# Edge sum of a graph layer: three fields a list in place of four, and VectorE's dependent operations spaced out

## The chip, the cores and the metric
One core of one Trainium2 chip runs the whole kernel. The metric is the device time of one execution in microseconds, the median over runs. The engines are TensorE (PE; PEld is its weight load), VectorE (DVE), ScalarE (ACT), GpSimd (POOL) and the sync engine (SP), which only issues transfers.

## The reference, cut to what matters
```python
# x: (6250, 256) f32; src, dst: (200000,) sorted by dst; edge_weight: (200000,) f32
xn = layernorm(x)
row, col = src, dst                       # edge_index = stack([src, dst])
gnn = segment_sum(edge_weight[:, None] * xn[col], row, num_segments=6250) + node_vec1
x = x + gnn + linear_attention(xn)        # four heads of 64, no softmax
x = x + mixture_of_experts(layernorm(x))  # 8 experts, the best 2 of each row
```
The edge sum is the part at issue: every edge adds its weight times the normalized row of `dst` to the row of `src`. Its weights are 32-bit floats and are kept in full in the sum.

## The kernel before, in words
The nodes are 49 tiles of 128 rows. `front` normalizes the rows, computes what the attention needs and prepares the edges; `edge_sum` adds up the edges and the attention; `stragglers`, `route` and `experts` follow. The change touches `front` and `edge_sum`.

**Edges as lists.** Since the edges are sorted by `dst`, those of one tile of `dst` lie together. Tile s of `dst` takes a window of 34 x 128 edges (CH = 34 per partition). Sorting one such window, called sort s, puts its edges into a table of 128 slots by NB = 49 tiles of `src`: one *list* per tile of dst, with one edge per slot and tile of src. It is done by one-hot products. `hot_t` (L1121) marks each edge's src tile, `base` (L845, 34 matmuls of 49 columns) counts the edges ahead, `rank_ahead` and `rank` (L1134 to L1145) give each edge its slot, `slots` (L1153) marks it. `values` (L1164) multiplies `hot_t` by each *field* of the edge, spread by ACT's `repeat_fields` (L981) over 1666 elements. `make_table` (L854) multiplies slots by values, 34 matmuls of FIELDS x 49 columns into one PSUM bank. ACT's `unpack` or `unpack_list` copies it out, and DVE's `part` (L1172, L1173) or `make_list` (L1180 to L1186) takes the fields apart.

**Fields.** There are four bf16 fields: END packs the two row numbers, and three hold the weight as a sum of bf16 parts, each the rest after the one before. In `front`, `weight_part` (POOL, five steps a chunk of seven tiles, one per node tile from APART on) makes the three parts with copies and subtractions, and `apart` (DVE, L547 to L559) the END field.

**Use of the lists.** The 49 tiles of dst make seven groups of seven. In a group four lists are *dense* (DENSE; src side is a one-hot block matrix times a resident window of xn rows) and three are *pick* lists (PICK; for them POOL gathers one row of xn per slot from DRAM, L817). For each group, all 49 tiles of src are computed, seven to a *unit*. So there are 7 x 49 node-tile steps in 49 units. In a step PE makes `blocks` of the next tile (L903, 12 bf16 matmuls of 128 columns) from DVE's `hots` (L1284) and `hot_w` (L1288, three weight parts), and `rows` (L911 and L915, seven f32 products of 256 columns); ACT copies the blocks out (`evacuate`, L1027) and spreads the next unit's entries (`take`, L1015 to L1021); DVE makes `pick_w` (`picks`, L1295) and adds the sum to the result (`add`, L1316).

**What sets the order.** Each engine runs one queue written out by hand: `schedule` runs eight sorts first (with the attention's `mix` between), then 42 units that each carry one more sort spread over their steps i = 0 to 6, then seven units without. In a unit's step i DVE does `picks` of tile i+1, `hots` with `hot_w` of tile i+2, `add` of tile i-1, then a piece of the sort: two `values` at 0, `part`, `in_row`, `rank_ahead` at 1, `rank` at 2, `make_list` and one `values` at 3, one at 4, `slots` at 5, `hot_tiles` at 6. PE does `base` at 0 and `make_table` at 6. Waits between engines are on counting semaphores; DVE also waits on its own semaphore where an operation reads what the one before wrote:
```python
dve.tensor_tensor(to ..., ALU.is_equal).then_inc(hot_done, 1)      # hots, L1284
dve.wait_ge(hot_done, t + 1)
dve.tensor_tensor(hot_w[i % SETS] ..., ALU.mult).then_inc(w_done, 1)  # L1288
```

Of the kernel before, what the change touches and what calls it, by code (L numbers as in the profile page):

```python
# [22 lines left out]
P = 128  # L23
# [20 lines left out]
FIELDS = 4  # L44
END, W = 0, 1
# [132 lines left out]
def front(nc, shared, edges, mixing, x, node_vec1, wq, wk, wv, wo, bo, kg, kb, vg, vb, xn_dram, xT_dram, src, dst, edge_weight,  # L178
# [25 lines left out]
    with ExitStack() as ctx:  # L204
# [7 lines left out]
        dst_t, src_t, dst_r, src_r = (sb(name, [P, UN, CH], I32) for name in ("dst_t", "src_t", "dst_r", "src_r"))  # L212
# [86 lines left out]
        def _(pool):  # L299
# [16 lines left out]
            def weight_part(c, n):  # L316

                at, part = slice(c * UN, (c + 1) * UN), n // 2
                if n == 0:
                    pool.wait_ge(e_in[c], 16 * 3 * UN)  # L320
                else:
                    pool.wait_ge(parts, 5 * c + n)
                if n % 2 == 0:
                    pool.tensor_copy(fields[:, W + part, at, :], weight[:, at, :]).then_inc(parts, 1)
                else:
                    pool.tensor_tensor(weight[:, at, :], weight[:, at, :], fields[:, W + part, at, :], ALU.subtract).then_inc(parts, 1)

            chunk_root(0)
            for t in range(NT):
                c, i = divmod(t, UN)  # L330
                root(t)
                if i == 2 and c + 1 < NC:
                    chunk_root(c + 1)
                for k in range(NC):
                    if 1 <= t - APART[k] <= 5:
                        weight_part(k, t - APART[k] - 1)
# [115 lines left out]
        def _(dve):  # L452
# [81 lines left out]
            def apart(c, m):  # L534

                at = slice(c * UN, (c + 1) * UN)
                if m == 0:
                    dve.wait_ge(e_in[c], 16 * 3 * UN)
                    if c > 0:
                        dve.wait_ge(kept, 2 * c)  # L540
                if m < 4:
# [8 lines left out]
                elif m == 4:  # L550
                    dve.wait_ge(cut, 4 * c + 3)
# [64 lines left out]
def edge_sum(nc, shared, edges, mixing, hot_w, xn_dram, xT_dram, base_dram, sum_dram, z_dram, Wg, bg, bias, wg, gb_row, G, NG, NT, N, D, HD):  # L616
# [16 lines left out]
    PARTS = FIELDS - W  # L633
# [5 lines left out]
    with ExitStack() as ctx:  # L639
# [23 lines left out]
        pair = sb("pair", [P, NB])  # L663
# [59 lines left out]
        listed = sem("listed"); pick_done = sem("pick_done"); rows_in = [sem(f"rows_in{i}") for i in range(SETS)]  # L723
# [82 lines left out]
        def _(pool):  # L806
            pool.wait_ge(mix_added, (GRP - 1) * BU)
            for t in range(NG * NT):
                g, b = divmod(t, NT)
                i = t % BU  # L810
                if b == 0:
                    pool.wait_ge(listed, 3 * PICK * (g + 1))
# [141 lines left out]
        def _(act):  # L954
# [22 lines left out]
            def repeat_fields(s, a, b):  # L977

                if later(s):
                    act.wait_ge(vals_done, 3 * s - (2 if b <= 2 else 1 if b <= 3 else 0))  # L980
# [17 lines left out]
            def unpack(s, j, par):  # L998
# [3 lines left out]
                act.copy(at[:, :, :, bass.ds(j, 1)].rearrange("p b f a -> p (f a) b"), table_ps).then_inc(unpacked, 1)  # L1002

            def unpack_list(s, n, q, par):
# [3 lines left out]
                if later(n):  # L1008
                    act.wait_ge(listed, 3 * n)
# [19 lines left out]
            def sort(s):  # L1029
                take_base(s)  # L1030
                repeat_fields(s, 2, 3)
                repeat_fields(s, 3, FIELDS)
# [6 lines left out]
                repeat_fields(s + 1, 0, 2)  # L1039

            def begin():
                act.wait_ge(unpacked, GRP)
                act.wait_ge(parted, DENSE)
                act.wait_ge(listed, 3 * PICK)
# [4 lines left out]
            def unit(g, k, odd, par, turn, more, after, q):  # L1049
# [4 lines left out]
                for i in range(BU):  # L1054
# [9 lines left out]
                    if more and i == 0:  # L1064
# [4 lines left out]
                        take_base(s)  # L1069
                        repeat_fields(s, 2, 3)  # L1070
                    if more and i == 1:
                        repeat_fields(s, 3, FIELDS)
                    if after and i in (2, 4):
                        if turned:
                            act.wait_ge(unpacked, (g + 2) * GRP)
                            act.wait_ge(parted, (g + 2) * DENSE)
                            act.wait_ge(listed, (g + 2) * 3 * PICK)
# [9 lines left out]
                    if more and i == 6:  # L1087
                        repeat_fields(s + 1, 1, 2)
# [8 lines left out]
            repeat_fields(0, 0, 2)  # L1097
# [3 lines left out]
        def _(dve):  # L1101
# [34 lines left out]
            def rank(s):  # L1136

                dve.wait_ge(ahead_done, 3 * s + 1)
                dve.wait_ge(same_done, s + 1)
                dve.tensor_tensor(ahead[:, :, 0:CH], ahead[:, :, 0:CH], same[:, :, :], ALU.add).then_inc(ahead_done, 1)  # L1140
                dve.wait_ge(ahead_done, 3 * s + 2)
                dve.tensor_tensor(ahead[:, :, 0:HALF], ahead[:, :, 0:HALF], ahead[:, :, NB + 1 - HALF:NB + 1], ALU.add).then_inc(ahead_done, 1)
                dve.wait_ge(ahead_done, 3 * s + 3)
# [23 lines left out]
            def part(s, j, par):  # L1167
# [5 lines left out]
                dve.tensor_scalar(both, both, P - 1, 0x3F80, ALU.bitwise_and, ALU.bitwise_or).then_inc(parted, 1)  # L1173

            def make_list(s, n, q, par):
# [5 lines left out]
                dve.tensor_scalar(row[:, :], raw[:, END, :].bitcast(I32), 23, None, ALU.logical_shift_right).then_inc(listed, 1)  # L1181
                dve.tensor_tensor(pair[:, :], raw[:, W, :], raw[:, W + 1, :], ALU.add).then_inc(listed, 1)
                dve.wait_ge(listed, 3 * n + 2)
                dve.tensor_tensor(place[par][:, bass.ds(q, 1), :].rearrange("p a b -> p (a b)"), row[:, :],
                                  first_row[:, bass.ds(s, 1)].broadcast_to([P, NB]), ALU.add)
                dve.tensor_tensor(weight[par][:, :, bass.ds(q, 1)].rearrange("p b a -> p (a b)"), pair[:, :], raw[:, W + 2, :], ALU.add).then_inc(listed, 1)  # L1186
# [56 lines left out]
            def sort(s):  # L1243
# [16 lines left out]
                values(s, 0, 2)  # L1260
# [4 lines left out]
                values(s, 2, 3)  # L1265
                if later(s):
                    add_mix(t + 1)
                values(s, 3, FIELDS)
                hot_tiles(s + 1)
                if later(s):  # L1270
                    add_mix(t + 2)
                slots(s)
                if s % 2 == 1:
                    part(s - 1, (s - 1) // 2, 0)
                elif s > 0:
                    make_list(s - 1, s // 2 - 1, s // 2 - 1, 0)

            def hots(t, i, odd, free):

                if free is not None:  # L1280
# [5 lines left out]
                                  of[:, i, 0:HOTS, :].unsqueeze(2).broadcast_to([P, HOTS, RUNS, REP]), ALU.is_equal).then_inc(hot_done, 1)  # L1286
                dve.wait_ge(hot_done, t + 1)
# [11 lines left out]
            def begin():  # L1299
# [3 lines left out]
                hots(0, 0, 0, None)  # L1303
                picks(0, 0, 0)
                hots(1, 1, 0, None)
                dve.wait_ge(saved, 16 * GRP)

            def unit(g, k, odd, par, turn, more, after, q):
# [13 lines left out]
                for i in range(BU):  # L1322
                    if i + 1 < BU:
# [792 lines left out]
```

## Time and profile before
| | us |
|---|---|
| median of 3 runs | 2283.73 (2283.42 to 2287.97) |
| profiled execution, its span from the first to the last instruction | 2536.7 |
| busy in it: PE, DVE, POOL, ACT | 2230.1, 1963.9, 1551.1, 1174.3 |
| mean granted TensorE clock | 0.929 |

The profiled execution has no time of its own beside its span. What lies around the span is not shown, and the span is 253 us longer than the median, so durations are read from single instructions and the span is not compared with the median directly. By time, the front runs to about 180 us, the eight sorts to 300, the 42 units with a sort to 1815, the seven without to 2060, routing and experts behind.

### The profile page before, as it was taken

How to read it: one execution, taken by the hardware profiler on the slowest of the kernel's cores; microseconds unless marked ns; L12 is line 12 of the kernel's file. 1: busy time of each engine (PE TensorE's matmuls, PEld its weight loads, DVE VectorE, ACT ScalarE, POOL GpSimd, SP SyncE). 2: the span in 40 equal slices, each digit the busy share in tenths (PEclk: the TensorE clock that was granted, in tenths of full speed). 3: DMA queues.
4: the chain of work that ended last, by engine and by line, in shares of the span. 5: the costliest groups of instructions: out<-in, count | busy, mean ns of one | idle time of the engine just before them, and what ended most of it. 6: DMA issues, size and time to landing. Idle time of an engine off the chain costs nothing. (4 is left out here: it accounts for less than half of the span.)

```text
span 2536.7 us, 45539 instructions
## 1 busy us (share of the span) xinstructions
PE 2230.1 (88%) x16549; PEld 1930.5 (76%) x16550; DVE 1963.9 (77%) x3350; ACT 1174.3 (46%) x1696; POOL 1551.1 (61%) x1356
## 2 busy tenths in 40 slices
PE   7987799999999899989988998999989944999993
PEld 4656687777887788778877787778877844999993
DVE  7989888788898788878877897879877757555552
ACT  2236544443444344434443454444322235888772
POOL 4750266666676566666665666666766612778883
PEclk9989999999999899989988999999999977999997
DMA  5532422222223222222222222222244453455555
GB/s 151 150 113 87 123 82 75 76 90 78 74 83 90 73 82 76 88 76 80 76 82 73 83 79 84 78 79 77 82 123 139 136 180 61 79 81 83 82 81 133
DMA packets 160931, 235.90 MB, mean 93 GB/s; under 512 B 54834, under 2 KB 121805, under 8 KB 160490
## 3 DMA queue, kind: packets, MB, share of 16 engines
q0 software_dynamic: 70896, 164.43, 25.4%
q1 hardware_dynamic: 75536, 55.29, 7.9%
q10 hardware_dynamic: 14314, 13.68, 1.6%
q8 instruction: 120, 1.97, 0.3%
q14 instruction: 65, 0.53, 0.1%
HBM read 186.46 MB, written 53.24 MB: 94 GB/s over the span
## 5 line engine op out<-in xcount | busy, mean ns | idle before, releaser
L817 POOL DMA_INDIRECT picked<-xn_dram,place x1029 | 1143.9, 1112 | 721.7 <-PE bank L915 289.8
L1027 ACT COPY stage<-bank 128x512 f32<-128x512 f32 x343 | 201.0, 586 | 796.9 <-remote 477.6
L915 PE MATMUL bank<-picked,pick_w 128*128 128x256 f32 x2058 | 518.4, 389 | 3.3 <-issue 3.3
L915 PEld LDWEIGHTS bank<-picked,pick_w 128*128 128x128 f32 x2058 | 405.7, 197 | 65.8 <-issue 5.2
L911 PE MATMUL bank<-window,stage 128*128 128x256 f32 x1568 | 416.9, 409 | 17.8 <-issue 12.8
L903 PE MATMUL bank<-hot_w,hots 128*128 128x128 bf16 x4116 | 312.0, 225 | 49.1 <-issue 44.8
L911 PEld LDWEIGHTS bank<-window,stage 128*128 128x128 f32 x1568 | 300.4, 202 | 65.1 <-issue 25.6
L1164 DVE TENSOR_TENSOR vals<-hot_t,field_rep 128x1666 bf16<-128x1666 bf16 x200 | 203.7, 1041 | 187.8 <-remote 180.2
L1288 DVE TENSOR_TENSOR hot_w<-hots,cur 128x1536 bf16<-128x1536 bf16 x343 | 328.6, 958 | 11.9
L903 PEld LDWEIGHTS bank<-hot_w,hots 128*128 128x128 bf16 x4116 | 267.1, 101 | 92.5 <-issue 54.5
L911 PE MATMUL bank<-stage 128*128 128x256 f32 x1176 | 315.5, 410 | 11.6 <-issue 10.4
L981 ACT COPY field_rep<-fields 128x1666 bf16<-128x1666 bf16 (+1 forms) x193 | 322.8, 1677 | 1.2 <-DVE vals L1164 1.2
L1284 DVE TENSOR_TENSOR hots<-ends,cur 128x1408 bf16<-128x1408 bf16 x343 | 303.1, 884 | 1.7 <-ACT cur L1021 1.7
L911 PEld LDWEIGHTS bank<-stage 128*128 128x128 f32 x1176 | 225.9, 203 | 49.0 <-issue 23.2
L1908 POOL DMA_INDIRECT sum_dram<-y,target x112 | 179.1, 1599 | 64.0 <-issue 31.1
L1316 DVE TENSOR_TENSOR acc<-acc,bank 128x256 f32<-128x256 f32 x343 | 142.3, 415 | 85.2 <-PE bank L915 44.7
L1295 DVE TENSOR_TENSOR pick_w<-hots,cur_w 128x384 f32<-128x384 bf16 x343 | 190.6, 556 | 0.2
L1899 POOL DMA_INDIRECT zin<-z_dram,token x112 | 115.5, 1031 | 83.4 <-POOLq L1600 49.6
L2002 PE MATMUL bank<-w,hh 128*128 x896 | 163.6, 282 | 1.1 <-DVE hl L2050 1.1
L854 PE MATMUL bank<-vals,slot 128*128 128x196 bf16 x1700 | 155.8, 249 | 4.9 <-issue 4.0
L854 PEld LDWEIGHTS bank<-vals,slot 128*128 128x128 bf16 x1700 | 147.9, 98 | 12.3 <-issue 5.8
L2002 PEld LDWEIGHTS bank<-w,hh 128*128 128x128 f32 x896 | 138.2, 189 | 1.4 <-issue 1.4
(253 smaller groups left out, 3414.6 us busy)
## 6 DMA issues: line engine op xcount, KB each, us to landing
picked<-xn_dram,place POOLq DMA_INDIRECT x1029
w<-in_L_ffn_W_dram SPq DMA_DIRECT2D x16, 512.0 KB, 8.9
xn_dram<-xn ACTq DMA_DIRECT2D x49, 128.0 KB, 1.9
xT_dram<-xT ACTq DMA_DIRECT2D x49, 128.0 KB, 2.1
base_dram<-acc SPq DMA_DIRECT2D x7, 896.0 KB
sum_dram<-acc SPq DMA_DIRECT2D x7, 896.0 KB
z_dram<-vals SPq DMA_DIRECT2D x7, 896.0 KB
out_dram<-sum_dram SPq DMA_DIRECT2D x1, 6250.0 KB, 21.8
```

Source lines behind the costliest of these rows:

```text
L817: pool.indirect_dma_start(out=picked[:, i % SETS * PICK + q, :], out_offset=None, in_=xn_dram, in_offset=bass.IndirectOffsetOnAxis(ap=plac ...
L854: mm = pe.matmul(table_ps, slot[:, c, :], vals[:, c, :, :], start=(c == 0), stop=(c == CH - 1))
L903: mm = pe.matmul(block_ps(pp, j), hot[buf][:, PICK + j, :], hot_w[buf][:, part, j, :], start=(part == 0), stop=(part == 2))
L911: pe.matmul(sum_ps[pp], block_sb[pp][:, j, :], window[par][:, j, :], start=(j == 0), stop=False)
L915: mm = pe.matmul(sum_ps[pp], pick_w[i % SETS][:, q, :], picked[:, i % SETS * PICK + q, :], start=False, stop=(q == PICK - 1))
L981: act.copy(field_rep[:, :, a:b, :], fields[:, a:b, bass.ds(s, 1), :].rearrange("p f a c -> p (a c) f").unsqueeze(3).broadcast_to([P, CH, b ...
L1027: act.copy(block_sb[pp].rearrange("p j c -> p (j c)"), banks[pp][:, :]).then_inc(a_copied, 1)
L1164: ins = dve.tensor_tensor(vals[:, :, f, :], hot_t[:, :, :], field_rep[:, :, f, :], ALU.mult)
L1284: dve.tensor_tensor(to[:, :, :].rearrange("p f (b r) -> p f b r", r=REP), ends[:, :, :].rearrange("p f (b r) -> p f b r", r=REP), of[:, i, ...
L1288: dve.tensor_tensor(hot_w[i % SETS][:, :, :, :].rearrange("p f g (b r) -> p f g b r", r=REP), to[:, AT_SRC:HOTS, :].rearrange("p g (b r) - ...
L1295: dve.tensor_tensor(pick_w[i % SETS][:, :, :].rearrange("p q (b r) -> p q b r", r=REP), hot[i % SETS][:, 0:PICK, :].rearrange("p q (b r) - ...
L2002: mm = pe.matmul(y_ps[i][:, n * D:(n + 1) * D], parts[a][:, c, n * P:(n + 1) * P], w, start=(m == 0), stop=(m == 3 * FC - 1))
```

## The change
A list has three fields: END, W and LOW. W is now the upper 16 bits of the weight, taken as they are. LOW holds the lower 16 bits with bit 14 taken out and a constant added (so that the pattern is an ordinary bf16 number); the bit taken out goes to the END field's free upper bit. After the table, DVE puts the bits together again (`halve`, `join`). For a dense list it then cuts the joined weight into the three bf16 parts that `hot_w` reads (`part_cut`, `part_weights`); for a pick list the joined word is the weight. The table's matmuls have 147 columns, and `hot_w` keeps its three parts.

In `front`:
```diff
-FIELDS = 4
+FIELDS = 3
 # weight_part (POOL): three steps in place of five
+high = weight[:, at, :]....bitcast(U16)[:, 1:2 * UN * CH:2]
+pool.tensor_copy(fields[:, W, at, :].bitcast(U16)..., high).then_inc(parts, 1)
+pool.wait_ge(cut, 6 * c + 2)
+pool.tensor_scalar(fields[:, LOW, at, :].bitcast(U16), low_k[:, :, :], float(LOWEST * P), None, ALU.add).then_inc(parts, 1)
+pool.wait_ge(cut, 6 * c + 6)
+pool.tensor_tensor(src_r[:, :, :], src_r[:, :, :], bit_e[:, :, :], ALU.add).then_inc(parts, 1)
 # apart (DVE), m == 0
+dve.tensor_scalar(low_k[:, :, :], bits, 0xBFFF, None, ALU.bitwise_and).then_inc(cut, 1)
+dve.tensor_scalar(bit_e[:, :, :], bits, 0x4000, 1, ALU.bitwise_and, ALU.logical_shift_left).then_inc(cut, 1)
 # m == 5
-dve.wait_ge(cut, 4 * c + 4)
+dve.wait_ge(parts, 3 * c + 3)
```
In `edge_sum`, ACT:
```diff
 def unpack(s, j, par):
-    act.copy(at[:, :, :, bass.ds(j, 1)]..., table_ps).then_inc(unpacked, 1)
+    act.copy(at[:, :, 0:2, bass.ds(j, 1)]..., table_ps[:, END:W + 1, :])
+    raw_free(s)
+    act.copy(raw[:, :, :], table_ps).then_inc(unpacked, 1)
 def unpack_list(s, n, q, par):
+    act.copy(weight[par][:, :, bass.ds(q, 1)]..., table_ps[:, W, :])
+    raw_free(s)
     act.copy(raw[:, :, :], table_ps).then_inc(unpacked, 1)
 # unit: repeat_fields(s, 1, 2) at i == 0, (s, 2, 3) at 1, (s + 1, 0, 1) at 3, none at 6
```
DVE:
```diff
+def halve(s):
+    dve.tensor_scalar(halves[:, 0, :], raw[:, LOW, :].bitcast(I32), 16, None, ALU.logical_shift_right)
+    dve.tensor_scalar(halves[:, 1, :], raw[:, END, :].bitcast(I32), 17, 0x4000, ALU.logical_shift_right, ALU.bitwise_and).then_inc(split, 1)
+def join(s, low_bits):
+    dve.wait_ge(split, splits_of(s) + 1)
+    return dve.scalar_tensor_tensor(out=low_bits, in0=halves[:, 0, :], scalar=float(-LOWEST * P), in1=halves[:, 1, :], op0=ALU.add, op1=ALU.add)
+def part_cut(s):
+    dve.wait_ge(split, splits_of(s) + 2)
+    dve.tensor_scalar(upper[:, :], raw[:, W, :].bitcast(I32), 8, 8, ALU.logical_shift_right, ALU.logical_shift_left).then_inc(split, 1)
+def part_weights(s, j, par):
+    dve.wait_ge(split, splits_of(s) + 3)
+    dve.tensor_tensor(second, upper[:, :].bitcast(F32), first, ALU.subtract)
+    dve.tensor_tensor(third, raw[:, W, :], upper[:, :].bitcast(F32), ALU.subtract).then_inc(parted, 1)
 # make_list: row and halve; place_list: join and place; pair and the sum into weight are gone
 # unit, step i
-picks(t + i + 1, ...)
-hots(t + i + 2, ...)        # with hot_w behind its own wait
-add(i - 1)
+hots(t + i + 2, ...)
+picks(t + i + 1, ...)
+rank_add(s), part_cut(s - 1)      # at i == 2
+weigh(t + i + 2, ...)             # hot_w
+rank_fold(s)                      # at i == 2
+add(i - 1)
+rank_sum(s)                       # at i == 2
```
The sort's other pieces in a unit's step, each behind `add`: one `values` at 0; at 1 `part` with `halve`, `in_row`, `part_join`, `rank_ahead`; at 3 `part_weights` or `make_list`, one `values`, `place_list`; one `values` at 4; `slots` and `hot_tiles` as before. In the eight sorts ahead of the units, `part` or `make_list` stands behind the last `values`, and `join`, `cut` and `part_weights` are spread between `hot_tiles`, `add_mix` and `slots`. The semaphore `listed` counts one per pick list in place of three, `parted` is counted by `part_weights`.

## Rows read from the trace of the kernel before
**Rows 1.** The page: its span, and part 1, busy time by engine.
```profile
span 2536.7 us, 45539 instructions
...
PE 2230.1 (88%) x16549; PEld 1930.5 (76%) x16550; DVE 1963.9 (77%) x3350; ACT 1174.3 (46%) x1696; POOL 1551.1 (61%) x1356
```

**Rows 2.** Stretches: length, busy PE, PEld, DVE, ACT, POOL, granted clock, DMA share, GB/s.
```profile
314.27:344.57 30.30, 30.22 (x251) 26.88 (x250) 27.34 (x39) 15.00 (x20) 19.75 (x19) 1.00 0.26 79
1714.02:1744.07 30.05, 30.05 (x252) 26.86 (x251) 28.28 (x42) 15.16 (x20) 20.51 (x19) 1.00 0.26 80
205.00:281.50 76.50, 59.65 (x501) 47.23 (x500) 75.37 (x119) 50.70 (x52) 0.00 (x0) 1.00 0.39 118
314.30:1815.00 1500.70, 1376.44 (x10501) 1189.87 (x10499) 1247.26 (x1815) 664.21 (x857) 977.59 (x880) 0.94 0.27 80
1815.00:2060.00 245.00, 224.13 (x1515) 196.34 (x1516) 172.24 (x343) 62.25 (x120) 152.16 (x138) 0.95 0.43 126
```

**Rows 3.** Timeline of PE, one unit: start, us, instructions.
```profile
1464.80 1.04 PE L845 MATMUL bank<-hot_t,before 128*128 128x49 bf16 x34
1465.68 0.83 PE L903 MATMUL bank<-hot_w,hots 128*128 128x128 bf16 x12
1466.35 1.95 PE L911 MATMUL bank<-window,stage 128*128 128x256 f32 x8
...
1469.43 0.83 PE L903 MATMUL bank<-hot_w,hots 128*128 128x128 bf16 x12
...
1488.16 3.06 PE L854 MATMUL bank<-vals,slot 128*128 128x196 bf16 x34
1491.07 0.83 PE L903 MATMUL bank<-hot_w,hots 128*128 128x128 bf16 x12
```

**Rows 4.** Timeline of PE, the start of another unit, with the idle time before.
```profile
1600.94 0.18 PE L845 MATMUL bank<-hot_t,before 128*128 128x49 bf16 x1 [1.17 <-issue]
```

**Rows 5.** Groups by form: PE at the blocks and at `base`, idle time and releasers.
```profile
L903 PE MATMUL bank<-hot_w,hots 128*128 128x128 bf16 x4116 | 312.0, 225 | 49.1 <-issue 44.8 <-DVE hot_w L1288 3.7
...
L845 PE MATMUL bank<-hot_t,before 128*128 128x49 bf16 x1700 | 73.8, 194 | 67.0 <-issue 61.2 <-DVE hot_t L1121 5.7
```

**Rows 6.** Timeline of DVE, the same unit and the next one's start.
```profile
1461.51 2.00 DVE L1164 TENSOR_TENSOR vals<-hot_t,field_rep 128x1666 bf16<-128x1666 bf16 x2 [7.00 <-remote]
...
1470.48 0.76 DVE L1140 TENSOR_TENSOR earlier<-earlier,same 128x1156 bf16<-128x1156 bf16 x1
1471.27 0.58 DVE L1142 TENSOR_TENSOR earlier<-earlier 128x816 bf16<-128x816 bf16 x1
...
1489.66 0.42 DVE L1316 TENSOR_TENSOR acc<-acc,bank 128x256 f32<-128x256 f32 x1 [1.01 <-PE bank L915]
1489.99 0.55 DVE L1295 TENSOR_TENSOR pick_w<-hots,cur_w 128x384 f32<-128x384 bf16 x1
1490.46 0.89 DVE L1284 TENSOR_TENSOR hots<-ends,cur 128x1408 bf16<-128x1408 bf16 x1
1491.38 0.96 DVE L1288 TENSOR_TENSOR hot_w<-hots,cur 128x1536 bf16<-128x1536 bf16 x1
1492.26 2.00 DVE L1164 TENSOR_TENSOR vals<-hot_t,field_rep 128x1666 bf16<-128x1666 bf16 x2
```

**Rows 7.** Timeline of DVE: small operations of a pick list.
```profile
1002.05 0.18 DVE L1181 TENSOR_SCALAR row<-raw 128x49 int32<-128x49 int32 x1
1002.15 0.20 DVE L1182 TENSOR_TENSOR pair<-raw 128x49 f32<-128x49 f32 x1
1002.38 0.21 DVE L1184 TENSOR_TENSOR place<-row,first_row 128x49 int32<-128x49 int32 x1
```

**Rows 8.** Groups by form: POOL's gathers and ACT's copy of a tile's fields.
```profile
L817 POOL DMA_INDIRECT picked<-xn_dram,place x1029 | 1143.9, 1112 | 721.7 <-PE bank L915 289.8 <-issue 269.3 <-DVE acc L1190 115.3
...
L1021 ACT COPY cur<-table 128x1472 bf16<-128x1472 bf16 x49 | 70.0, 1428 | 0.0
```

**Rows 9.** Groups by form: DVE in the front, one bit operation of `apart`.
```profile
L547 DVE TENSOR_SCALAR dst_t<-dst_i 128x238 int32<-128x238 int32 x7 | 2.0, 279 | 0.6 <-DMA weight<-in_edge_weight_dram 0.5
```

More of the change, by code:

```diff
@@ L43 @@
 UNROLL = 7
-FIELDS = 4
-END, W = 0, 1
+FIELDS = 3
+END, W, LOW = 0, 1, 2
 LOWEST = 32
@@ L1172, in part, with splits_of, part_join @@
                 dve.tensor_scalar(dst, both, 0x7F80, None, ALU.bitwise_and)
-                dve.tensor_scalar(both, both, P - 1, 0x3F80, ALU.bitwise_and, ALU.bitwise_or).then_inc(parted, 1)
+                dve.tensor_scalar(both, both, P - 1, 0x3F80, ALU.bitwise_and, ALU.bitwise_or)
+                halve(s)
+            def splits_of(s):
+                g, k = divmod(s, GRP)
+                return 3 * (g * DENSE + (k + 1) // 2) + g * PICK + k // 2
+            def halve(s):
[4 more added lines that the diff above has]
+                return dve.scalar_tensor_tensor(out=low_bits, in0=halves[:, 0, :], scalar=float(-LOWEST * P), in1=halves[:, 1, :], op0=ALU.add, op1=ALU.add)
+            def part_join(s):
+                join(s, raw[:, W, :].bitcast(U16)[:, 0:2 * NB:2]).then_inc(split, 1)
+            def part_cut(s):
[3 more added lines that the diff above has]
+                dve.wait_ge(split, splits_of(s) + 3)
+                first, second, third = (table[par][:, :, at:at + DENSE][:, :, bass.ds(j, 1)].rearrange("p b a -> p (a b)")
+                                        for at in (AT_SRC + DENSE, AT_SRC + 2 * DENSE, AT_SRC + 3 * DENSE))
+                dve.tensor_tensor(second, upper[:, :].bitcast(F32), first, ALU.subtract)
+                dve.tensor_tensor(third, raw[:, W, :], upper[:, :].bitcast(F32), ALU.subtract).then_inc(parted, 1)
             def make_list(s, n, q, par):
@@ L1180, in make_list, with place_list @@
                 dve.tensor_scalar(col, col, P - 1, 0x3F80, ALU.bitwise_and, ALU.bitwise_or)
-                dve.tensor_scalar(row[:, :], raw[:, END, :].bitcast(I32), 23, None, ALU.logical_shift_right).then_inc(listed, 1)
-                dve.tensor_tensor(pair[:, :], raw[:, W, :], raw[:, W + 1, :], ALU.add).then_inc(listed, 1)
-                dve.wait_ge(listed, 3 * n + 2)
+                dve.tensor_scalar(row[:, :], raw[:, END, :].bitcast(I32), 23, 0xFF, ALU.logical_shift_right, ALU.bitwise_and)
+                halve(s)
+            def place_list(s, n, q, par):
+                low_bits = weight[par][:, :, :].rearrange("p b q -> p (b q)").bitcast(U16)[:, 2 * q:2 * NB * PICK:2 * PICK]
+                join(s, low_bits)
                 dve.tensor_tensor(place[par][:, bass.ds(q, 1), :].rearrange("p a b -> p (a b)"), row[:, :],
-                                  first_row[:, bass.ds(s, 1)].broadcast_to([P, NB]), ALU.add)
-                dve.tensor_tensor(weight[par][:, :, bass.ds(q, 1)].rearrange("p b a -> p (a b)"), pair[:, :], raw[:, W + 2, :], ALU.add).then_inc(listed, 1)
+                                  first_row[:, bass.ds(s, 1)].broadcast_to([P, NB]), ALU.add).then_inc(listed, 1)
             def add_mix(t):
@@ L1303, in begin @@
                 hots(0, 0, 0, None)
+                hots(1, 1, 0, None)
+                weigh(0, 0, 0)
                 picks(0, 0, 0)
-                hots(1, 1, 0, None)
+                weigh(1, 1, 0)
                 dve.wait_ge(saved, 16 * GRP)
@@ L1334, in unit @@
                         hots(t + i + 2, i + 2 - BU, 1 - odd, t + i + 2)
+                    if i + 1 < BU:
+                        picks(t + i + 1, i + 1, odd)
+                    elif after:
+                        picks(t + BU, 0, 1 - odd)
+                    if more and i == 2:
+                        rank_add(s)
+                        if odd == par:
+                            part_cut(s - 1)
+                    if i + 2 < BU:
+                        weigh(t + i + 2, i + 2, odd)
+                    elif after:
+                        weigh(t + i + 2, i + 2 - BU, 1 - odd)
+                    if more and i == 2:
+                        rank_fold(s)
                     if i > 0:
```

111 lines of the change are left out of this document (67 added, 44 removed).

## The prediction
> **What bounds the kernel now.** First the page: the span is 2536.7 us, PE is busy for 88% of it and DVE for 77% [rows 1]. The profiled execution is 253 us longer than the median of 2283.73 us, so I first ask where that lies. By stretches [rows 2], PE has the most to do in the edge sum's steady part, 314 to 1815 us: 1376 of 1501 us. That part is 42 units of seven node tiles, 35.7 us each on average. In the PE's order of time for one unit [rows 3] the reader is to see that each step starts where the one before ends: the 34 matmuls of `base` take 0.88 us (1464.80 to 1465.68), a tile takes 3.75 us (1465.68 to 1469.43), the 34 matmuls of the table 2.91 us (1488.16 to 1491.07). 7 x 3.75 + 0.88 + 2.91 is 30.0 us for a unit without a pause. Nine of the 41 units that can be measured from one `base` to the next are like this; of those the first took 30.30 us and the last 30.05, PE busy throughout and its granted clock 1.00 [rows 2]. The others are longer by what the next view shows: PE stands in the middle of `base`, up to 1.17 us at a time, with "issue" as the reason [rows 4], and the granted clock of the whole stretch is 0.94 [rows 2]. The grouped idle times say the same: of PE's 67.0 us at `base` 61.2 are issue, of its 49.1 us at the blocks 44.8, and only 5.7 and 3.7 us are DVE's [rows 5].
>
> So 42 x (35.7 - 30.0) = 240 us of the profiled span are stalls of issue and the clock behind them, about the 253 us by which this execution is longer than the median. I take it that the measured runs go without most of them, at the bare 30.0 us a unit, and apply the differences below, all taken at unstalled durations, to the median.
>
> Close behind PE is DVE. From one unit's first pair of vals to the next (1461.51 to 1492.26) DVE ran 30.75 us, 1.10 of them a wait for PE's sum (1.01 us, and the 0.09 by which its operations otherwise overlap): 29.65 us of its own work with a dense list [rows 6]. A pick list has make_list, five small operations and a wait, in place of two: 4 x 0.11 + 0.23 against 0.22 [rows 7], so 30.1 us. PE has 30.0: a tie. From start to start, 2.60 us of each tile are acc 0.33, pick 0.47, hots 0.92 and hot_w 0.88 [rows 6].
>
> **The change, part by part.** *The table.* 196 columns become 147. Start to start, a matmul of 196 columns takes 2.91/34 = 86 ns, one of 128 columns 0.67/12 = 56 ns [rows 3]. 147 lie between, on the line at 67 ns (49 columns less at 0.43 ns a column is 21 ns). Per unit 34 x 21 = 0.72 us; the bounds are 0 (it costs what 196 do) and 1.0 us (56 ns). 42 x 0.72 = **30.2 us**, on the path if PE bounds; bounds 0 and 43.
> The Trainium skill, page "TensorE: Matmul & The Clock Gate", section "Back-to-back issue gap", gives a sustained 81 ns per weight load and matmul at 128 columns and 131 ns at 512, which speaks against this part: an estimate on its line is 0.13 ns a column, 6.4 ns a matmul, 9 us for the 42 units instead of 30.
>
> *DVE in a unit.* One vals less: two in a row are busy for 2.00 us, so -0.96. Hots is no longer followed by the hot_w that reads it. hot_w starts 0.92 after hots, which was busy for 0.89, whereas hots starts 0.08 before the pick ahead of it ends (1490.46 against 1490.54) [rows 6]; so 0.12 less on each of seven tiles, -0.8. The rank's two gaps (add to fold: busy 0.76, start to start 0.79) close likewise, -0.24. Added: a dense list gets halve twice, join, cut and two subtractions, six small operations; a pick list gets halve twice and join and loses pair and weights. Neighbours of 49 elements start 0.10 us apart, behind a wait 0.23 [rows 7], which are the bounds; I take 0.11 (near the lower end), since other work stands between the dependent ones: +0.66 dense; for a pick list +0.11 and the wait of 0.12 gone, 0. DVE becomes 29.6 - 2.0 + 0.66 = 28.3 or 30.1 - 2.0 = 28.1 us. PE becomes 29.3 us and is now alone the bound. DVE's saving is thus worth nothing in the sum; it buys slack of about 1 us.
> *ACT.* One field copy of 1666 elements less, for a dense list a raw copy of 147 more, for a pick list one of 49, each smaller than a tile's copy of 1472 elements at 1.43 us [rows 8]. ACT is busy 664 of 1501 us [rows 2]: hidden by PE. Without that cover a dense unit would pay at most those 1.43 us.
> *Order and new waits.* hots, which waits for `a_done`, now stands ahead of pick. It waits for blocks two PE steps back, so pick is not held. weigh comes one pick, and once a unit also the rank's add, later (0.5 to 1.4 us). PE wants it a step later, 3.75 us. The part's end (`parted`) moves from DVE's step 1 to step 3. At a group's last unit ACT waits for it before `take`, with the evacuation of the tile after the next queued behind: three ACT copies, the largest of 1.43 us [rows 8], behind an event at the end of PE's step 2, and PE needs the last of them one tile and one set of blocks later, 3.75 + 0.67 = 4.4 us. It just fits even with all three at 1.43; a microsecond late would cost 6 x 1 us. The fields' wait at step 0 is for one field rather than two and is met earlier. POOL's gathers wait for the pick lists, placed in step 3 as before; POOL works 1112 ns for each of 21 a unit [rows 8], 23.4 us, hidden also under 29.3.
> *The sort phase ahead of the units*, eight sorts. In the stretch shown DVE is busy for 75.4 of 76.5 us [rows 2], so here DVE counts: -0.96 each, and +0.66 on four dense lists, 0 and one wait less on the others: 8 x 0.96 - 4 x 0.66 + 0.4 = **5.4 us less**. The rank is not pulled apart here. If each small operation of a dense list cost 0.23 instead, 3 us of it would go.
> *The front.* Two bit operations are new in each of seven chunks. Such an operation is busy for 0.28 us [rows 9], 0.20 net of the overlap of 0.08; I count 14 x 0.20 = **2.8 us more**, as if nothing hid them. POOL has three weight parts a chunk in place of five. DVE's END field now waits for POOL's last part, which POOL does one tile before DVE comes to it: cost 0, or as a far bound a POOL instruction's 1.11 us [rows 8] seven times, 7.8 us.
> *The last seven units* make no table. PE is busy 224 of 245 us there, DVE 172 [rows 2]; the reordering frees DVE only: 0. Routing and experts are untouched.
> Sum: -30.2 - 5.4 + 2.8 = -32.8; 2283.7 - 32.8 = **2251 us**. Against the profiled execution's own span the same sum gives 2504, if its stalls stay as they are.
>
> **The rivals.**
> *More than the table.* If DVE with its 30.1 us rather than PE paced the measured runs, the unit was some tenths longer than 30.0 and DVE's 1.6 us count. For: the tie, and that DVE's work is spread unevenly over the steps. Against: the profiled span less its stalls, 2536.7 - 240 = 2297, already exceeds the median, and PE hardly waits for DVE [rows 5]. Half a microsecond more a unit is 21 us: 2230.
> *The table's saving is given back.* If measured runs carry the stalls of issue too, a shorter table leaves the sequencer less time to get ahead, and `base`, which comes one tile later with the shortest matmuls, stands longer by the 0.72. Only sort and front are left: 2281. For: stalls sit in `base` [rows 4]. Against: the agreement of 240 with 253.
> *The rate of pairs.* If weight load and matmul together set the step, and fewer columns bring a third of the expected, the sum is -9 - 2.6, 2272. The rows say no: 56 ns at 128 columns against 86 at 196, and 26 ns at 49 (0.88/34) [rows 3]. This is the time by the page's rule named above; the trace disagrees with its 81 ns.
> *Slower.* The same stalls, but crossing a point: a unit that runs clean now gets a stall in `base`, the clock falls behind it, and the unit takes the 35.7 of the mean. Each costs 6 us, so from six of the nine clean units on the gain is gone; all nine give 2251 + 54 = 2305.
>
> **How the numbers follow.** Forecast 0.74 (its own range 2241 to 2262, from the bounds of table and small operations), more than the table 0.10, given back 0.08, rate of pairs 0.03, slower 0.05. No change is within 0.2%, 4.6 us, about what a measurement of this kernel can tell. Given back straddles that line: faster 0.88, same 0.07, slower 0.05. The range leaves out the slow end and most of given back: 2232 to 2270.
>
> **What would show it.** Right: L854 at 147 columns with 34 in about 2.2 us; a clean unit of 29.3 us from `base` to `base` with PE without a pause; hots to pick 0.80; DVE idle for about 1 us in such a unit; the sort phase about 5 us shorter. Wrong: a table of 34 matmuls still at 2.9; clean units at 30; PE waiting for w_done, a_copied or `parted`; a clean unit below 29 us cannot be, and a gain above 45 us would say that DVE was the bound.

## The result, and the profile after

The changed kernel takes 2365.14 us (2364.49 to 2372.38) against 2284.78 us for the kernel before: a ratio of 1.036 (95% interval 1.034 to 1.038), 80 us **slower**. The prediction was 2251 us, 34 us faster, with 0.05 on slower.

The profiled execution of the changed kernel has a span of 2363.5 us, close to its median, unlike that of before with its 2536.7 [rows 1]. A second profiled execution of the kernel before, taken with the experiments, has 2287.4 us and is the one to compare with. First the page of the changed kernel: span, part 1, and the two groups of part 5 that matter.

```profile
span 2363.5 us, 45680 instructions
...
PE 2103.7 (89%) x16549; PEld 1851.8 (78%) x16550; DVE 1904.5 (81%) x3503; ACT 1092.0 (46%) x1703; POOL 1675.8 (71%) x1342
...
L824 POOL DMA_INDIRECT picked<-xn_dram,place x1029 | 1270.6, 1235 | 426.6 <-issue 306.6
L922 PE MATMUL bank<-picked,pick_w 128*128 128x256 f32 x2058 | 522.2, 391 | 96.2 <-DMA picked<-xn_dram,place 96.2
```

The same two groups, by form, in the second profile of the kernel before:

```profile
L817 POOL DMA_INDIRECT picked<-xn_dram,place x1029 | 1187.8, 1154 | 434.8 <-issue 299.5 <-DVE acc L1190 115.3 <-PE bank L915 19.9
```

What to see: PE now waits 96 us for gathered rows (17 us in that second profile; none is shown in the first one's groups). And a gather takes 1235 ns of POOL instead of 1154, 81 ns on each of 1029, which is 83 us. That is the whole loss, if POOL is the engine that sets the pace. It is. Between two gathers POOL stands for 0.30 us with "issue" as the reason; with it, POOL is full. Stretches of the changed kernel (the steady part; a short unit; a long one), with the columns of [rows 2]:

```profile
305.60:1645.40 1339.80, 1245.64 (x10251) 1098.21 (x10250) 1171.73 (x1892) 583.50 (x838) 1074.61 (x859) 0.96 0.30 87
1577.60:1607.00 29.40, 29.40 (x253) 26.24 (x252) 28.73 (x47) 14.17 (x21) 23.00 (x22) 1.00 0.32 95
1607.00:1645.40 38.40, 32.51 (x251) 28.34 (x250) 28.31 (x45) 14.31 (x20) 31.84 (x22) 0.91 0.26 76
```

and the steady part in the second profile of the kernel before:

```profile
309.80:1560.80 1251.00, 1239.68 (x10252) 1096.39 (x10250) 1216.67 (x1780) 652.50 (x838) 987.87 (x856) 1.00 0.32 93
```

POOL is busy for 1074.6 us, and 859 times 0.305 us of issue make 262 more: 1337 of 1340 us. In the kernel before it is 988 + 261 = 1249 of 1251 us. **Both kernels are bound by POOL's gathers**; PE works 1240 of 1251 us before and 1246 of 1340 after. These 41 units took 88.8 us more (30.5 to 32.7 us each); the sorts ahead of them 5.4 less (from the first `base` to the first unit's, 126.0 to 120.6), the front about 1 more, and what comes behind the last `base` 8.6 less (726.6 to 718.1): together 76 us, the difference of the two spans.

Where the time sits shows in the order of time of one long unit. POOL:

```profile
1549.83 3.73 POOL L824 DMA_INDIRECT picked<-xn_dram,place  x1 [0.30 <-issue]
1553.86 3.11 POOL L824 DMA_INDIRECT picked<-xn_dram,place  x1 [0.30 <-issue]
1557.28 4.58 POOL L824 DMA_INDIRECT picked<-xn_dram,place  x1 [0.30 <-issue]
1562.16 0.95 POOL L824 DMA_INDIRECT picked<-xn_dram,place  x1 [0.30 <-issue]
```

VectorE meanwhile:

```profile
1549.31 1.05 DVE L1193 TENSOR_TENSOR vals<-hot_t,field_rep 128x1666 bf16<-128x1666 bf16 x1
1550.26 0.33 DVE L1218 SCALAR_TENSOR_TENSOR weights<-halves 128x49 uint16<-128x49 int32 x1
1550.38 0.25 DVE L1250 TENSOR_TENSOR place<-row,first_row 128x49 int32<-128x49 int32 x1
1550.50 0.89 DVE L1357 TENSOR_TENSOR hots<-ends,cur 128x1408 bf16<-128x1408 bf16 x1
1551.31 0.56 DVE L1373 TENSOR_TENSOR pick_w<-hots,cur_w 128x384 f32<-128x384 bf16 x1
1551.77 0.96 DVE L1366 TENSOR_TENSOR hot_w<-hots,cur 128x1536 bf16<-128x1536 bf16 x1
1552.64 0.42 DVE L1396 TENSOR_TENSOR acc<-acc,bank 128x256 f32<-128x256 f32 x1
1552.97 1.05 DVE L1193 TENSOR_TENSOR vals<-hot_t,field_rep 128x1666 bf16<-128x1666 bf16 x1
...
1555.19 0.96 DVE L1366 TENSOR_TENSOR hot_w<-hots,cur 128x1536 bf16<-128x1536 bf16 x1
...
1556.39 2.50 DVE L1182 TENSOR_TENSOR slot<-iota_j,rank_rep 128x2176 bf16<-128x2176 bf16 x2
1558.80 0.90 DVE L1357 TENSOR_TENSOR hots<-ends,cur 128x1408 bf16<-128x1408 bf16 x1
1559.60 0.57 DVE L1373 TENSOR_TENSOR pick_w<-hots,cur_w 128x384 f32<-128x384 bf16 x1
1560.07 0.97 DVE L1366 TENSOR_TENSOR hot_w<-hots,cur 128x1536 bf16<-128x1536 bf16 x1
```

and PE at the end of it:

```profile
1556.04 1.95 PE L918 MATMUL bank<-stage 128*128 128x256 f32 x8
1563.88 2.90 PE L922 MATMUL bank<-picked,pick_w 128*128 128x256 f32 x6 [5.89 <-DMA picked<-xn_dram,place]
1566.57 1.49 PE L910 MATMUL bank<-hot_w,hots 128*128 128x128 bf16 x12
```

A gather alone takes 0.95 us. The one that starts at 1549.83, inside vals, ends at 1553.56: that is 0.83 us after the end of hot_w (1551.77 + 0.96 = 1552.73), the first VectorE operation behind which something else than a run of two-SBUF-operand operations follows (acc reads PSUM). The next, from 1553.86, ends at 1556.97, 0.82 us behind the next hot_w (whose end is 1556.15). The third starts in slot and ends at 1561.86, 0.82 behind the third. Three gathers take 11.4 us where 2.9 would do. PE stands for 5.89 us, and the six f32 products behind that take 2.90 us instead of 1.46 and the blocks 1.49 instead of 0.83, about twice the time, at the lower of the clock's two levels: it fell behind PE's pause (the mean is 0.91 over this unit too, 1539.5 to 1577.6 us; 1.00 over the short one). There are 52 gathers above 2.2 us in the changed kernel and 2 in the second profile of the kernel before. The 52 take 193 us together. The other 977 have a mean of 1103 ns, less than the 1151 of the kernel before without its 2: the long ones are the whole loss.

The rule holds over the whole trace. Of the 543 gathers of the changed kernel that take more than 0.975 us, 528 end 0.82 us, give or take 0.015, after the end of some VectorE operation; moved by 0.2 to 0.5 us against VectorE, either way, 19 would on average. In the second profile of the kernel before it is 541 of 543. The Trainium skill, page "GPSIMD Engine Reference", section "1. Specifications", says that GpSimd's SBUF interfaces are shared with VectorE and contend with instructions that run in a 2-port mode or have two SBUF inputs. The trace agrees: gathers that start in acc (one operand in PSUM), in a `tensor_reduce` or in a pause take 0.95 us.

### The profile page after: what moved, and what is told of

It reads as the page before. It is cut to its first block and busy times, and to the rows that moved or that the text cites. A ratio compares the mean times of both kernels' runs of the same rounds, so it can differ in the third digit from the quotient of the medians.

```text
span 2363.5 us, 45680 instructions
## 1 busy us (share of the span) xinstructions
PE 2103.7 (89%) x16549; PEld 1851.8 (78%) x16550; DVE 1904.5 (81%) x3503; ACT 1092.0 (46%) x1703; POOL 1675.8 (71%) x1342
## 5 line engine op out<-in xcount | busy, mean ns | idle before, releaser
L824 POOL DMA_INDIRECT picked<-xn_dram,place x1029 | 1270.6, 1235 | 426.6 <-issue 306.6
L918 PE MATMUL bank<-window,stage 128*128 128x256 f32 x1568 | 384.5, 388 | 0.0
L918 PEld LDWEIGHTS bank<-window,stage 128*128 128x128 f32 x1568 | 285.4, 192 | 31.4 <-ACT stage L1046 0.5
L910 PE MATMUL bank<-hot_w,hots 128*128 128x128 bf16 x4116 | 294.7, 223 | 2.9 <-issue 1.6
L918 PE MATMUL bank<-stage 128*128 128x256 f32 x1176 | 288.8, 389 | 0.0
L988 ACT COPY field_rep<-fields 128x1666 bf16<-128x1666 bf16 x151 | 243.0, 1615 | 0.0
L918 PEld LDWEIGHTS bank<-stage 128*128 128x128 f32 x1176 | 214.3, 192 | 23.7 <-ACT stage L1046 0.5
L1193 DVE TENSOR_TENSOR vals<-hot_t,field_rep 128x1666 bf16<-128x1666 bf16 x150 | 160.3, 1069 | 1.6 <-PE bank L861 1.5
L2087 PE MATMUL bank<-zh,w1h 128*128 128x256 f32 x448 | 133.4, 298 | 3.0 <-issue 1.9
L861 PE MATMUL bank<-vals,slot 128*128 128x147 bf16 x1700 | 127.1, 235 | 4.8 <-issue 3.9
```

The costliest lines, as they stand in the source:

```text
L824: pool.indirect_dma_start(out=picked[:, i % SETS * PICK + q, :], out_offset=None, in_=xn_dram, in_offset=bass.IndirectOffsetOnAxis(ap=plac ...
L910: mm = pe.matmul(block_ps(pp, j), hot[buf][:, PICK + j, :], hot_w[buf][:, part, j, :], start=(part == 0), stop=(part == 2))
L918: pe.matmul(sum_ps[pp], block_sb[pp][:, j, :], window[par][:, j, :], start=(j == 0), stop=False)
L988: act.copy(field_rep[:, :, a:b, :], fields[:, a:b, bass.ds(s, 1), :].rearrange("p f a c -> p (a c) f").unsqueeze(3).broadcast_to([P, CH, b ...
L2087: mm = pe.matmul(hid_ps(i, c), ww[b][:, k * F + c * P:k * F + (c + 1) * P], zz[a][:, k, :], start=(m == 0), stop=(m == 5))
```

## The experiments

Eleven runs, the first of them the kernel before itself; the changed kernel stands beside them. Ratios are to the kernel before, run beside each. "Over 2.2" counts gathers longer than 2.2 us over the whole trace; "mean" is a gather's mean in it. A trace has 1029 gathers, with a third of them 343.

| kernel | median us | ratio (95% interval) | mean ns | over 2.2 |
|---|---|---|---|---|
| before, once more | 2284.91 | 0.9996 (0.9979 to 1.0012) | 1154 | 2 |
| changed | 2365.14 | 1.0361 (1.0342 to 1.038) | 1235 | 52 |
| changed, pause behind hots in every tile | 2264.84 | 0.9918 (0.9901 to 0.9934) | 1140 | 12 |
| changed, hot_w at once behind hots | 2385.18 | 1.0453 (1.0435 to 1.047) | 1254 | 19 |
| before, new order of hots, pick, hot_w | 2279.24 | 0.9973 (0.9961 to 0.9985) | 1151 | 10 |
| changed, a third of the gathers | 2230.52 | 0.9750 (0.9731 to 0.9768) | 1360 | 48 |
| before, a third of the gathers | 2259.47 | 0.9887 (0.9870 to 0.9904) | 1159 | 0 |
| changed, old order in a unit | 2288.84 | 1.0012 (0.9995 to 1.0029) | 1161 | 13 |
| changed, pause behind place | 2257.67 | 0.9878 (0.9860 to 0.9896) | 1126 | 3 |
| changed, pauses behind vals and slot only | 2295.80 | 1.0035 (1.0020 to 1.0049) | 1167 | 23 |
| changed, pauses behind hots and place | 2258.00 | 0.9868 (0.9852 to 0.9885) | 1126 | 5 |
| changed, old order, pause behind place | 2280.00 | 0.9962 (0.9948 to 0.9976) | 1153 | 6 |

**The kernel before, profiled once more.**

> The kernel before, unchanged, profiled once more, since its first profiled execution was 253 us longer than its runs. If the stalls of issue in base belong to that one execution: span 2275 to 2290 us, units of about 30 us. If they belong to every profiled execution of this kernel: about 2530 us again.

Measured: span 2287.4 us, no unit above 31.5. So the stalls of issue in `base` belonged to that one profiled execution, as the prediction took it. But in that execution POOL had slack, since PE was late, and its gathers were not what was waited for. That is what hid the bound.

**A pause behind hots.**
```diff
 hots(t + i + 2, ...)
+dve.wait_ge(hot_done, t + i + 3)
```


> The changed kernel with one addition: VectorE waits for its own hots right behind it, ahead of pick, so that it pauses once a tile; order and fields stay as changed. Theory (POOL's gathers can only finish when VectorE pauses or works on a PSUM operand; the spacing took the pauses away): no gather above 2.2 us (the changed kernel has 72 of 3.1 to 4.6 us in its steady part), PE's wait for gathered rows from 96 us to under 10 us, units of 29.3 to 30 us, time 2245 to 2265 us. Rival 1 (the new order, with hot_w later, starves PE): stays at 2365. Rival 2 (join with its strided 16-bit output blocks POOL): long gathers stay at the pick lists, 2340 or more.

(The 72 in this text is a slip: 72 is the count above 1.7 us in the steady part; above 2.2 there are 52, and of those 51 take 3.1 to 4.6.) Measured: 2264.84 us, at the upper edge of the theory's; PE's wait for rows is 20 us, a bit more than named, and 12 gathers remain above 2.2. The order of the changed kernel is not at fault by itself, and join, which stayed, need not cost anything. Adding a wait made the kernel 100 us faster.

**hot_w directly behind hots.**
```diff
 hots(t + i + 2, ...)
+weigh(t + i + 2, ...)
 picks(t + i + 1, ...)
-weigh(t + i + 2, ...)
```


> The changed kernel with hot_w directly behind hots again and pick behind it, so the dependent pause is back once a tile; three fields, join and the spaced rank stay. Theory (missing pauses): as the kernel with the added pause, 2245 to 2265 us. Rival 2 (three fields, join and the small operations do it): stays at 2340 to 2365.

A miss: 2385.18 us, slower than the changed kernel, though the pause is there and only 19 gathers are above 2.2. Of these, 18 are held over join and place and let in at the pause behind hots. The ordinary ones have grown: the 1010 below 2.2 have a mean of 1224 ns. Four rows of POOL and VectorE of this kernel:

```profile
906.58 1.49 POOL L824 DMA_INDIRECT picked<-xn_dram,place  x1 [0.30 <-issue]
908.37 1.45 POOL L824 DMA_INDIRECT picked<-xn_dram,place  x1 [0.30 <-issue]
```
```profile
906.29 0.96 DVE L1366 TENSOR_TENSOR hot_w<-hots,cur 128x1536 bf16<-128x1536 bf16 x1
...
907.97 1.04 DVE L1193 TENSOR_TENSOR vals<-hot_t,field_rep 128x1666 bf16<-128x1666 bf16 x1
```

The gather from 906.58 ends at 908.07, 0.82 us after hot_w (907.25); that from 908.37 ends at 909.82, 0.81 after vals (909.01). Here a gather is held only until the end of the operation in which it starts, but it starts early in one again and again: 718 of 1029 gathers take more than 0.975 us in this trace, 543 in the kernel before. So there are two costs, not one: the ordinary hold to the end of the current operation, which depends on where in VectorE's order POOL's steps fall, and the long ones. My theory of missing pauses told only of the second.

**The new order alone.**
```diff
-picks(...); hots(...)      # hot_w behind its wait inside hots
+hots(...); picks(...); weigh(...)
```


> The kernel before with the new order of hots, pick and hot_w alone; four fields, rank and lists as before. Theory: gathers above 2.2 us appear, PE waits for rows, 2340 us or slower (VectorE is fuller with four vals, so it pauses still less). Rival 2 (the fields): 2284 us, no long gathers, and VectorE's saved 0.8 us a unit is worth 0 to 10 us.

The theory missed here too: 2279.24 us, 5 us faster than before, with 10 gathers above 2.2. Nine of the 10 take 4.03 us, held from the sort's operations of step 1 over hots, pick and hot_w, so long holds arise with four fields as well; but only gathers of 1.3 and 1.6 us follow them, no second long one, and the kernel is not slower. What hurts needs both halves of the change.

**A third of the gathers, in both kernels.**
```diff
-for q in range(PICK):
+for q in range(1):
     pool.indirect_dma_start(...)
```


> The changed kernel with one of a tile's three gathers; the three pick products all read that one gathered row set, so two thirds of the picked rows are wrong data. Theory (POOL's gathers, not PE, set the pace of the changed kernel): PE at its own floor, all units at about 29.4 us, time about 2226 us. If PE or VectorE with the new order set it: about 2365 us.

> The kernel before with one of a tile's three gathers, leaving out the same as the other. Theory (the kernel before, too, is held by its gathers, though little): all units at 30.0 us, about 2264 us, so that the difference to the changed kernel with a third of the gathers is 30 to 40 us: what three fields are worth where gathers don't count. Rival (three fields bring nothing on PE): the two equal.

Measured: 2230.52 and 2259.47 us, 29 us apart where 30 to 40 were expected. 1200 us out of the steady part of each, changed kernel first:

```profile
310.00:1510.00 1200.00, 1200.00 (x10190) 1071.11 (x10188) 1159.37 (x1881) 580.05 (x835) 389.80 (x286) 1.00 0.12 35
```
```profile
310.00:1510.00 1200.00, 1200.00 (x10000) 1073.07 (x9999) 1182.15 (x1733) 635.99 (x819) 326.20 (x280) 1.00 0.12 34
```

PE is busy for all 1200 us in both; the units are 29.4 us (29.37 to 29.5) and 30.0. So PE and VectorE of the changed kernel do nearly what the prediction's sum said: 0.62 us less a unit (30.01 to 29.39) where 0.72 was forecast, 26 us for 42 units in place of 30. The kernel before had 25 us (2285 to 2259) of gathers on its path, the changed one 135. The gathers left are held as before, in the changed kernel even longer (mean 1360 ns, 48 above 2.2), and it costs nothing, since POOL works only 390 of the 1200 us.

**Three fields with the old order.**
```diff
-hots(...); picks(...); rank_add(s); part_cut(s - 1); weigh(...); rank_fold(s)
+picks(...); hots(...); weigh(...)
 add(i - 1)
-rank_sum(s)
+rank(s); part_cut(s - 1)
```


> The changed kernel with the old order in a unit: pick, hots, hot_w behind its wait, and the rank in one piece; three fields and the operations that put the weight together stay. If the new order made the gathers long: no gather above 2.2 us but behind join, and 2250 to 2270 us. If the three fields with join and place do it: long gathers in the pick units, 2300 us or more.

Between the two: 2288.84 us, no change that can be measured. PE's 30 us are not realized, since POOL cannot go faster: its gather's mean is 1161 ns, and 21 x (1.161 + 0.305) = 30.8 us a unit (30.66 measured). Of the 13 above 2.2, 11 are held over join and place.

**One pause, behind place.**
```diff
 place_list(s - 1, lists_before(g + 1, q), q, 1 - par)
+dve.wait_ge(listed, lists_before(g + 1, q) + 1)
```


> The changed kernel with one wait of VectorE for its own place, right behind it, in each unit with a pick list, 18 in all. In the changed kernel's trace the chains of long gathers all begin with one that is held while vals, join, place and hots run into each other. Theory (this seam starts them): gathers above 2.2 us fall from 72 to under 10 and the time to 2290 us or less, by 18 waits of 0.12 us. Rival (the missing pause behind hots in every tile is what counts): few long ones go, 2340 or more.

Measured: 2257.67 us with 3 gathers above 2.2. Eighteen waits undo 107 us. The same seam as above, POOL and VectorE:

```profile
763.79 1.58 POOL L824 DMA_INDIRECT picked<-xn_dram,place  x1 [0.30 <-issue]
765.67 1.14 POOL L824 DMA_INDIRECT picked<-xn_dram,place  x1 [0.30 <-issue]
767.12 0.94 POOL L824 DMA_INDIRECT picked<-xn_dram,place  x1 [0.30 <-issue]
```
```profile
763.28 1.04 DVE L1193 TENSOR_TENSOR vals<-hot_t,field_rep 128x1666 bf16<-128x1666 bf16 x1
764.23 0.32 DVE L1218 SCALAR_TENSOR_TENSOR weights<-halves 128x49 uint16<-128x49 int32 x1
764.35 0.24 DVE L1250 TENSOR_TENSOR place<-row,first_row 128x49 int32<-128x49 int32 x1
764.63 0.89 DVE L1357 TENSOR_TENSOR hots<-ends,cur 128x1408 bf16<-128x1408 bf16 x1
```

Place ends at 764.59 and hots starts at 764.63, not 764.47. The gather gets in and ends at 765.37, rather than 3.7 us after its start. That is 0.78 us after place's end and 0.82 after join's (764.23 + 0.32 = 764.55), and so in all 18 units (0.774 to 0.787 and 0.813 to 0.827). By the rule of 0.82 us it is let in at join's end, 0.08 us before hots starts. In the changed kernel hots started before join's end (1550.50 against 1550.59), and none of 18 gathers got in there. So the wait opens the seam; whether it is the gap of 0.04 us that does it, or that hots is not under way yet, no run tells.

This run also shows the chain. The later seams, vals to hots and slot to hots, have no wait in this kernel, and yet of the 19 gathers of 3.1 us and the 14 of 4.6 one each is left, and neither is in a unit with a pick list. With the first hold gone, the later ones do not arise.

**Pauses later, none at place.**
```diff
 values(s, 2, 3)                          # step 4
+dve.wait_ge(vals_done, FIELDS * s + 3)
 slots(s)                                 # step 5
+dve.wait_ge(slot_done, s + 1)
```


> The changed kernel with two waits of VectorE for its own work per unit, behind the vals of step 4 and behind slot of step 5, none at place. In the changed kernel long gathers come in chains: 3.7 us over join and place, then 3.1 from inside vals, then 4.6 from inside slot (by the trace 18, 19 and 14 of 52). Theory (one held gather sets the start of the next so that it is held too): the 18 at place stay, those of 3.1 and 4.6 go; about 18 x 2.8 = 50 us over the kernel with the pause at place, 2300 us give or take 15. Rival (the long ones have causes of their own): the 3.1s and 4.6s that remain show it.

2295.80 us, in the range named. 18 gathers of 3.75 us over join and place stay and none of 4.6; of those near 3.1 one is left, in the last units, and the other four of the 23 lie in the sorts, the first unit and the switch to the last ones. After the first one POOL is nearly free again, here with the two VectorE operations around the pause of step 4:

```profile
1109.85 3.75 POOL L824 DMA_INDIRECT picked<-xn_dram,place  x1 [0.30 <-issue]
1113.91 0.98 POOL L824 DMA_INDIRECT picked<-xn_dram,place  x1 [0.31 <-issue]
1115.19 1.09 POOL L824 DMA_INDIRECT picked<-xn_dram,place  x1 [0.30 <-issue]
```
```profile
1113.04 1.03 DVE L1193 TENSOR_TENSOR vals<-hot_t,field_rep 128x1666 bf16<-128x1666 bf16 x1
1114.10 0.89 DVE L1357 TENSOR_TENSOR hots<-ends,cur 128x1408 bf16<-128x1408 bf16 x1
```

The gather from 1113.91 starts at the old point, 0.16 us before vals ends (1114.07), and is let in at that end (1114.89 less 0.82), behind which hots now starts 0.03 us later. So the two pauses sit at the very seams where the long gathers of 3.1 and 4.6 us missed, and this run does not tell the theory from its rival. It shows that the holds over place arise without the later ones, and what 18 of them cost: 38 us over the kernel with the pause at place, 2.1 us each where 2.8 was named.

With the run before it, the order of events in the changed kernel is this. The hold over place ends 0.82 us after hot_w, the next gather starts 0.30 us later, always at the same point of the following vals, 0.16 to 0.17 us before its end (19 of 19), and is held again.

**Pauses behind hots and place; old order with the pause at place.**

```diff
 # the changed kernel with the pause behind place
 hots(t + i + 2, ...)
+dve.wait_ge(hot_done, t + i + 3)
```


> The changed kernel with the pause behind place and the one behind hots in every tile. Theory (only the seams where gathers miss count): no gather above 2.2 us, about 2257 us like the pause at place alone; if more pauses help the ordinary gathers as well, 2245 us.

```diff
 # three fields with the old order
 place_list(s - 1, lists_before(g + 1, q), q, 1 - par)
+dve.wait_ge(listed, lists_before(g + 1, q) + 1)
```


> Three fields with the old order in a unit (2289 us), with the pause behind place. Theory: its 13 gathers above 2.2 us go, some 15 to 20 us are gained, 2270 us; the rest of the distance to 2258 is VectorE's and POOL's ordinary holding.

2258.00 us: more pauses do no more than the 18 (2257.67), and 5 gathers above 2.2 remain where none was expected. 2280.00 us: 9 to 11 us gained (by the medians, by the ratios) where 15 to 20 were expected; the new order is worth about 20 us (0.9962 to 0.9878) once the seam is mended, through ordinary holds (mean 1153 against 1126 ns), not through VectorE's saved time.

## Why the prediction was wrong

**The step that failed** is in the part on order and new waits: "POOL works 1112 ns for each of 21 a unit, 23.4 us, hidden also under 29.3." It is wrong twice. First, a gather costs its duration and the 0.30 us of issue behind it. The row was there: 269.3 us of issue in the idle time of the same group [rows 8]. 21 x 1.417 is 29.8 us, level with PE's 30.0 and above the 29.3 that the change was to reach. At that, the forecast would have been about 10 us from the units (42 x 0.24) in place of 30, with POOL as the bound. Second, the duration is not a constant: it holds the time for which VectorE keeps POOL waiting, 0.95 us alone and 1.15 on average before. It moves with VectorE's order, and the change reorders VectorE. With 1.235 it came to 21 x 1.54 = 32.3 us a unit; in the 41 units the mean was 1.252, and they took 32.7 us.

**Which of the changes did it.** Neither alone: three fields with the old order 2289, the new order with four fields 2279, both 2365 us. (Neither of the first two has the rank pulled apart; that it does no harm by itself is to be seen only from the runs with pauses, which keep it.) Three fields bring the seam vals, join, place, hots without a pause; the new order takes the pause between hots and hot_w, which would have ended the hold 2.6 to 2.9 us after the gather's start (the 11 of the run with the old order) and broken the chain. That the seam starts it, and that the later holds hang on the first, is shown by the 18 waits alone; how the old order breaks the chain is read from the traces and was not tested by itself.

**Point by point.**
- *That the stalls of issue are not in the measured runs* (240 of 253 us): right, by the second profile. What I did not ask is what a profile in which PE is late says about the slack of the others: nothing. POOL's waits for PE, 289.8 us in [rows 8], came from those stalls, and are 19.9 us without them.
- *The table*: right. The 34 matmuls take 2.26 us start to start (1600.95 to 1603.21), 66 ns each:
```profile
1600.95 2.42 PE L861 MATMUL bank<-vals,slot 128*128 128x147 bf16 x34
1603.21 0.83 PE L910 MATMUL bank<-hot_w,hots 128*128 128x128 bf16 x12
...
1605.66 1.46 PE L922 MATMUL bank<-picked,pick_w 128*128 128x256 f32 x6
```
  The 67 ns of the prediction is a slip: 86 less its 21 is 65, which is what its 0.72 us and its 2.2 us go by. The line of [rows 3] holds; the saving is 0.65 us a unit (2.91 to 2.26). The sustained 81 ns at 128 columns of the Trainium skill's page "TensorE: Matmul & The Clock Gate", section "Back-to-back issue gap", and with it the estimate of 9 us, is refuted by this row and by the pair with a third of the gathers, which is 29 us apart.
- *A clean unit of 29.3 us*: right, 29.40 above.
- *DVE*: right in size. hots to pick is 0.80 us (1558.80 to 1559.60), as forecast, against 0.92 to hot_w before. With a third of the gathers VectorE is busy for 28.4 us a unit in place of 29.6, and stands for 1.0, as forecast. "It buys slack" was wrong: it was paid for by POOL. The page "VectorE: DVE Perf Modes" of the Trainium skill, section "The DRAIN you can't avoid", says of eight copies in a row that the semaphore between them costs nothing extra. Here it costs 0.12 us: hots to pick is 0.80 us in the changed kernel and 0.92 with the pause behind hots, the same two operations.
- *Sort phase* -5.4: -5.4 measured between the two profiles. *Front* +2.8: +1.2 there, but among the profiles the first `base` lies anywhere from 179.4 to 185.4 us, so this is not resolved. *Behind the last* `base`: forecast 0 beside the table, measured -8.6; the cause is open. With a third of the gathers this part takes 717.0 us in the kernel before and 718.8 in the changed one, so that the 8.6 us seem to hang on the gathers.
- *The rivals*: "more than the table" took DVE for the bound, "slower" and "given back" took stalls of issue, which the second profile does not have, and "the rate of pairs" falls by the table's 66 ns. None named POOL. The slower one had about the right size of loss a unit (6 us; the long units lose 4 to 9) by accident only.

**The best version** is the changed kernel with the pause behind place: 2257.67 us, 1.2% faster than before (interval 1.0 to 1.4%), and the same with both pauses. The 27 us left to the 2230.52 of a third of the gathers are POOL's.

## What to carry to other kernels

Work out every engine's time for one round of the steady state from start to start, issue gaps with it, and do so in an execution whose span agrees with the measured median; an engine that is 71% busy by the page, as POOL in the changed kernel, can be at 100% of its path. Before a change packs VectorE more densely, look at what POOL does beside it: if it issues gathers, its instruction's duration is a measure of VectorE's holds, and a wait that looks wasted may be the gap through which it gets in. Try a single wait at the seam where the longest gather begins, before undoing anything.

## What the runs showed of the hardware

- A gather of 128 rows holds POOL for 0.95 us alone. In the changed kernel 543 of 1029 take more than 0.975 us. They start, with few exceptions, while VectorE is in an operation with two SBUF operands, and 528 of them end 0.82 us after the end of an operation: 470 after that of the one in which they start.
- Not every end lets a gather in. In the changed kernel none of the 18 that came up to the seams vals to join, join to place, and place to hots got in, and having missed these they missed hots to pick and pick to hot_w as well, though 154 others got in at hots to pick and 42 at pick to hot_w. But of the held gathers that fit the 0.82 us none, in any of the thirteen profiles, passed an end behind which VectorE stood for 0.03 us or more, or one beside an operation with an operand in PSUM. Why a boundary between running operations serves at one time and not at another stays open; no run here tells it.
- POOL's gathers and VectorE lock to each other, so that the same holds return at the same point in unit after unit: in the changed kernel the 18 start 0.53 to 0.57 us before the end of vals, the 19 of 3.1 us 0.16 to 0.17 before it, and the 14 of 4.6 us 0.41 before the end of the first slot operation. So the order counts beside the number of operations: the changed kernel with a pause behind hots takes 2265 us with pick ahead of hot_w and 2385 with pick behind it.
